# A two-layer graph network: wide product in the setup, rows broadcast by loads, the Rayleigh quotient on VectorE, one convolution moved to the drain between the layers, and a new order of the last batches

## What is computed

```python
h = relu(layernorm(x));  x = x + L0(h, adj)
h = relu(layernorm(x));  x = x + L1(h, adj)

def L0(x, adj):                      # 8 Euler steps, linear in h
    h = x @ fc_in_w.T + fc_in_b
    for _ in range(8):
        f = sigmoid(alpha) * 0.5 * (adj @ h - h) + h @ (w * clip(d, 0, 1) @ w.T) - h + x0
        h = h + f / 8
    return h

def L1(x, L, adjacency):
    lam_max = eigvalsh(L)[-1] + 1e-8
    h = relu(layernorm(((2 * L / lam_max - I) @ x) @ Wc + bc)) + x
    q, k, v = h @ Wq, h @ Wk, h @ Wv          # 4 heads of 32
    attn = softmax(where(adjacency > 0, q @ k.T / sqrt(32), -1e9))
    x2 = layernorm(h + (attn @ v) @ Wo + bo)
    return layernorm(x2 + gelu(x2 @ W1 + b1) @ W2 + b2)
```

## Time and profile before

| | us |
|---|---|
| median of 3 runs | 900.57 (898.94 to 904.41) |
| the profiled execution | 900.85 |
| its span, first to last instruction | 899.0 |
| PE busy | 850.9 (95%) |
| PEld busy | 715.9 (80%) |
| DVE busy | 649.3 (72%) |
| ACT busy | 539.1 (60%) |
| POOL busy | 327.2 (36%) |

### The profile page before, as it was taken

How to read it: one execution, slowest core, us unless ns; L and a number is a source line. 1 busy time by engine, 2 the same in 40 slices (tenths; PEclk the granted TensorE clock), 3 DMA queues, 4 the chain that set the end, 5 groups by cost and what they waited for, 6 DMA issues and landing times.

```text
span 899.0 us, 19047 instructions
## 1 busy us (share of the span) xinstructions
PE 850.9 (95%) x6765; PEld 715.9 (80%) x6765; DVE 649.3 (72%) x2110; ACT 539.1 (60%) x1234; POOL 327.2 (36%) x426
## 2 busy tenths in 40 slices
PE   6999999999999999988999999999999999989993
PEld 5779999999999888986777777777777777767873
DVE  6865555545453545635889999999999988987996
ACT  3134343434343232314888888988888888886884
POOL 3211111111111132301444455555555454424986
PEclk9799999999999999999999999999999999999997
DMA  3000000000000000230555554344455555410122
GB/s 103 0 1 25 12 12 13 12 13 13 12 12 13 12 24 1 76 66 3 139 143 142 142 141 127 105 119 123 98 140 143 141 142 137 112 37 1 48 71 71
DMA packets 46429, 61.73 MB, mean 69 GB/s; under 512 B 3568, under 2 KB 21247, under 8 KB 46335
## 3 DMA queue, kind: packets, MB, share of 16 engines
q1 hardware_dynamic: 46034, 60.38, 26.0%
q10 hardware_dynamic: 300, 0.13, 0.1%
HBM read 39.53 MB, written 20.97 MB: 67 GB/s over the span
## 4 chain that ended last, share of the span: by engine, by line
PE 29%; DVE 11%; issue 6%; ACT 4%; DMA 3%; SPq 1%; POOL 0%; DVEq 0%; ACTq 0%; POOLq 0%
PE bank L1769 7%; PE bank L1789 5%; PE bank L1831 4%; PE bank L1756 4%; DVE prob L1938 3%; PE bank L1509 3%; PE bank L1491 2%; DMA q_stack<-bounce_k 2%; ACT prob L1881 2%; PE bank L359 1%; DVE z_std L308 1%; DVE probT L1925 1%; PE bank L363 1%; DVE stats_b L285 1%; PE bank L1472 1%
## 5 line engine op out<-in xcount | busy, mean ns | idle before, releaser
L1881 ACT ACTIVATE prob<-prob,low 128x512 f32<-128x512 f32 x256 | 184.0, 719 | 31.0 <-DVE low L1938 29.0
L1938 DVE CUSTOM_DVE_ANT_0 prob<-bank,mask 128x512 f32<-128x512 f32 x256 | 171.0, 683 | 10.0 <-PE bank L1756 7.6
L1769 PE MATMUL bank<-ident,prob 128*128 128x128 f32 x1024 | 157.6, 276 | 1.0 <-ACT probT L1864 0.8
L1769 PEld LDWEIGHTS bank<-ident,prob 128*128 128x128 f32 x1024 | 120.6, 141 | 40.5 <-issue 29.2
L1756 PE MATMUL bank<-k_stack,q_stack 128*128 128x512 f32 x256 | 124.1, 486 | 9.8 <-DVE low L1938 8.0
L1864 ACT ACTIVATE probT<-bank 128x512 f32<-128x512 f32 x176 | 103.7, 589 | 21.7 <-PE bank L1769 21.5
L820 PE MATMUL bank<-B_hi,halves 128*128 128x384 f32 x384 | 107.2, 342 | 1.6 <-DVE halves L1183 1.1
L791 PE MATMUL bank<-halves,P3T_hi 128*128 128x256 f32 x512 | 95.4, 288 | 3.4 <-DVE halves L1201 2.2
L610 POOL TENSOR_SCALAR var_eps<-mv 128x4 f32<-128x4 f32 x16 | 3.6, 226 | 243.7 <-DVE mv L1127 243.7
L791 PEld LDWEIGHTS bank<-halves,P3T_hi 128*128 128x128 f32 x512 | 81.7, 194 | 5.8 <-DVE halves L1201 2.5
L820 PEld LDWEIGHTS bank<-B_hi,halves 128*128 128x128 f32 x384 | 70.7, 189 | 4.6 <-DVE halves L1183 2.0
(11 more groups left out here) (265 smaller groups left out, 1994.0 us busy)
## 6 DMA issues: line engine op xcount, KB each, us to landing
k_stack<-bounce_q SPq DMA_DIRECT2D x64, 256.0 KB, 4.6
q_stack<-bounce_k SPq DMA_DIRECT2D x64, 256.0 KB, 7.6
bounce_q<-k_parts SPq DMA_DIRECT2D x16, 512.0 KB, 2.8
bounce_k<-q_parts SPq DMA_DIRECT2D x16, 512.0 KB, 3.0
x_in<-in_x_dram SPq DMA_DIRECT2D x16, 256.0 KB, 2.8
out_dram<-probT SPq DMA_DIRECT2D x16, 256.0 KB, 2.3
y<-in_adj_dram SPq DMA_DIRECT2D x4, 256.0 KB, 3.7
W1s<-in_L_gnn_W_dram SPq DMA_DIRECT2D x1, 128.0 KB, 2.3
```

Source lines behind the costliest of these rows:

```text
L1769: last = pe.transpose(psum[2 + u % 2][:, mt * P:(mt + 1) * P], prob[u % RING][:, mt * P:(mt + 1) * P], ident[:, :])
L1881: act.activation(prob[u % RING][:, :], prob[u % RING][:, :], ACT.Exp, bias=low[:, u % TURNED:u % TURNED + 1], scale=-1.0, accum_out=row_su ...
L1938: dve.tensor_tensor_reduce(prob[u % RING][:, :], psum[u % 2][:, :], mask[:, u // HEADS, :], 1.0, 3e38, ALU.add, ALU.min, low[:, u % TURNED ...
```

## The change

Six edits, made together. (1) P2 is made product by product (all hi*hi of the four tiles, then hi*lo, then lo*hi), so that it can start before the rests of P are there; half of the rounding of P moves from ACT to DVE; S is added up later; POOL's sum `PT` is gone. (2) U starts as the columns 0, 1 and row sum, and is split; PE multiplies it as a weight of 3 columns with `PT_hi` and `PT_lo` (12 matmuls of 512 columns), which gives all three rows at once. (3) The nine vectors are loaded by DMAs that read the row for each of the 128 partitions. (4) S*v goes to VectorE: DVE writes v on four diagonals, PE with a weight of ones turns that into v on all partitions, DVE multiplies each tile of S with it and sums; all of it in pair 5. (5) The convolution of batch 2 is done in pair 8, in f32, and not in round 1; `v_product` of batch 0 goes to pair 7. (6) At the end DVE takes `z3_moments(15)` ahead of `finish(13)`, and POOL makes the last `y_be3` one batch earlier.

```diff
@@ the loads (SP)
-                        sp.dma_start(one.row_in[:, n, :], row.rearrange("(o d) -> o d", o=1)
+                        sp.dma_start(one.bc_all[:, n, :], row.rearrange("(o d) -> o d", o=1).broadcast_to([P, D])
@@ GpSimd: setup and pair
-                pool.wait_ge(PT_lo_ready, NT)
-                pool.tensor_tensor(out=PT[:, :, :], in0=PT_parts[0][:, :, :].bitcast(F32), ...
-                    if p == LAM_PAIR:
+                    x_and_bias(2 * p, 0)
+                    if p == LAM_PAIR - 1:
                         for b in range(2):
                             h_scales(pool, one, b, b)
-                    x_and_bias(2 * p, 0)
@@ TensorE: P2, the sums of rows, the spread rows
-                pe.wait_ge(Pn_lo_ready, NT)
-                pe.wait_ge(PT_lo_ready, NT)
-                for mt in range(NT):
-                    node_power(mt, PT_parts, P2_psum)
+                pe.wait_ge(Pn_hi_ready, NT // 2)
+                pe.wait_ge(P_ready, 2 * NT + NT // 2)
+                pe.wait_ge(PT_hi_ready, NT)
+                for n, (left, right) in enumerate(products(Pn_parts, PT_parts)):
+                    for mt in range(NT):
...
                 pe.wait_ge(S_ready, 2)
                 pe.wait_ge(B_step, 1)
                 pe.matmul(SQ_BANK[:, 0:1], ones[:, :], row_sum[:, :], start=True, stop=True).then_inc(setup_psum, 1)
-                pe.wait_ge(PT_sum_ready, 1)
-                pe.wait_ge(U_ready, 2)
-                for nt in range(NT):
-                    for k in range(NT):
-                        last = pe.matmul(psum[6][:, nt:nt + 1], PT[:, k, nt * P:(nt + 1) * P], U[:, k, 1:2], ...
+                pe.wait_ge(U_ready, GROUP + 2)
+                for k in range(NT):
+                    for n, (u, p) in enumerate(products(U_parts, PT_parts)):
+                        last = pe.matmul(psum[6][0:GROUP, :], u[:, k, :], p[:, k, :], ...
-                pe.wait_ge(one.rows_loaded, 16 * ROWS)
-                for c in range(3):
-                    pe.matmul(psum[4 + c][:, 0:cols], ones[0:1, :], row_flat[:, c * N:c * N + cols], ...
@@ TensorE: early
-                    if step == (0, "T1a"):
-                        pe.wait_ge(square_ready, NT * SQUARINGS)
+                    if step == (-1, "T1b"):
+                        pe.wait_ge(Sv_step, NT)
                         for nt in range(NT):
-                            for k in range(NT):
-                                last = pe.matmul(SQ_BANK[:, nt:nt + 1], S[:, k, nt * P:(nt + 1) * P], v[:, k:k + 1],
+                            last = pe.matmul(SQ_BANK[:, nt * P:(nt + 1) * P], ones[:, :],
+                                             one.convT[:, nt * P:(nt + 1) * P], start=True, stop=True)
-                    if step == (0, "Y1_0"):
-                        pe.wait_ge(Sv_step, 3)
+                    if step == (-1, "C3b"):
+                        pe.wait_ge(Sv_step, 2 * NT + 2)
-                    if step == (2, "Y1_1"):
+                    if step == (1, "Y0_1"):
                         pe.wait_ge(one.q_lo_ready, 1)
                         v_product(pe, one, SQ_BANK, 0)
+                    if step == (2, "Y1"):
+                        pe.wait_ge(one.v_copied, 1)
+                        for k in range(NT // 2):
+                            conv(pe, one, SQ_BANK, 2, 0, k)
+                    if step == (2, "Y1_1"):
+                        for k in range(NT // 2, NT):
+                            conv(pe, one, SQ_BANK, 2, 0, k)
@@ VectorE: setup
+                for t in range(NT // 2, NT):
+                    dve.tensor_copy(Pn_parts[0][:, t, :], Pn[:, t, :]).then_inc(P_ready, 1)
                 power_out(4)
-                dve.wait_ge(adjT_ready, NT)
-                dve.tensor_tensor(out=S[:, :, :], in0=A[:, :, :], in1=adjT[:, :, :], op=ALU.add)
...
-                turned_lo(0, P2T_parts, NT + 1)
+                for mt in range(NT):
+                    turned_lo(mt, P2T_parts, NT + mt + 1)
...
-                for c in range(3):
-                    dve.wait_ge(one.rows_spread, c + 1)
-                    dve.tensor_copy(one.bc_all..., psum[4 + c][:, 0:cols])
+                dve.tensor_scalar(U_rows[:, :], psum[6][0:GROUP, :], ident[0:GROUP, 0:1], None,
+                                  ALU.add).then_inc(rows_ready, 1)
@@ VectorE: early (SV_PLACES = {"T2b": (0, 1), "C0b": (2,), "C1b": (3,)})
-                    if step == (0, "T1a"):
-                        for b in range(2):
-                            y_moments(dve, one, b)
+                    if step == (-1, "y0"):
+                        y_moments(dve, one, 0)
+                    if step == (-1, "y1"):
+                        y_moments(dve, one, 1)
+                    if step == (-1, "v"):
+                        for nt in range(NT):
+                            dve.tensor_scalar(one.convT[:, nt * P:(nt + 1) * P], ident[:, :], v[:, nt:nt + 1], ...
+                    if p == LAM_PAIR - 1 and at in SV_PLACES:
+                        dve.wait_ge(lam_psum, 1)
+                        for nt in SV_PLACES[at]:
+                            dve.tensor_tensor_reduce(diagonal[...], S[:, nt, :], SQ_BANK[:, :], 1.0, 0.0, ALU.mult,
+                                                     ALU.add, Sv[:, nt:nt + 1]).then_inc(Sv_step, 1)
@@ layer 1: round 1 has no convolution and no split_h any more
-                    if within(r, 1, BATCH - 2):
+                    if within(r, 2, BATCH - 2):
                         split_h(r + 1, 1 - s)
-                        if AT_CONV <= u < AT_CONV + NT and within(r, 0, BATCH - 2):
+                        if AT_CONV <= u < AT_CONV + NT and within(r, 2, BATCH - 2):
-                            conv_out(act, one, A_BANK, r + 1)
+                            conv_out(act, one, A_BANK if r > 1 else psum[7], r + 1)
@@ the end
+        if b < BATCH - 1:
+            shifted_y(pool, b)
+        if b == BATCH - 2:
+            shifted_y(pool, b + 1)
         inverse_root(pool, b, mv3[b % 2], mv3_ready, ve3, rstd3[b % RING], pool3, z3_std_ready, b - RING + 1,
...
-                finish(dve, BATCH - 3)
                 z3_moments(dve, BATCH - 1)
-                finish(dve, BATCH - 2)
-                finish(dve, BATCH - 1)
+                for b in range(BATCH - 3, BATCH):
+                    finish(dve, b)
```

112 lines of the change are left out of this document (63 added, 49 removed).

## The result

The changed kernel takes 887.79 us (median of 4, 887.13 to 889.18), the kernel before 899.76 beside it: ratio 0.9854, 95% interval 0.9818 to 0.9889. The two profiled executions are 887.13 and 900.85, their spans 885.3 and 899.0.

What follows compares the result with a forecast made beforehand. It took PE, then DVE, then PE to bound the setup, PE layer 0's pairs, ACT round 1. Terms -3.7 + 0.9 - 6.7 + 0.9 - 1.2 - 0.8 = -10.6 from 900.85 gave 890.25, median 890.0; range 887 to 894.

Steps and rivals of the forecast that it cites:

- rival D: Whole kernel: every term comes at its good bound, -13.6 in sum, 887.0 us and somewhat below; chance 0.08.
- Setup, -3.7: Setup: first squaring 4.5 us earlier, less a third of 2.4 for a possible clock loss, so -3.7.
- bounds -2.1 and -4.9: Setup term's limits: -2.1 with the clock loss of 2.4 in full, -4.9 with none and a better chain of powers.
- Pair 5, +0.9: Pair 5 pays for the quotient's added PE and DVE work: +0.9 us, bounds 0.3 and 2.8.
- Pair 6, -6.7: Pair 6 loses S*v (3.48 us) and Y1 falls from 9.07 to 5.85: -6.7, bounds -5.5 and -6.8.
- Pair 7, +0.9: Pair 7 takes v_product, where PE has no wait to hide it: +0.9 us.
- Pair 8, 0: Pair 8: both halves of batch 2's convolution, 1.72 us each, hidden in PE's waits, with 0.4 to spare.
- Round 1, -1.2: Round 1 without batch 2's convolution: ACT goes on at 434.75, not 435.94, so -1.2, bounds -0.5 and -2.0.
- End, -0.8: End: last finish at 893.7 to 894.2, not 894.76, so -0.8 us, bounds -0.3 and -1.1.
- Loads, 0: Row loads: nine rows of 64 KB each instead of 0.5, nothing in front waits for them, cost nothing.
- B: Setup: the clock falls once or twice more, giving 891.6 or 894 us; chance 0.20.
- E: Attention rounds: round 1's change starts them in another, longer phase; slower, 911 us at 1.5 a round; chance 0.02.

Runs made afterwards that it cites:

- e2: The kernel before with only the broadcast loads of the rows in place of the spreading matmuls and their copies: 897.38 us against 901.09, ratio 0.9953.
- e3: The kernel before with only the edit of the quotient (S*v to VectorE, in pair 5): 892.68 us against 901.09, ratio 0.9901.
- e12: The changed kernel with the addition of S back in its old, early place on VectorE: 889.35 us, ratio 0.9884 to the kernel before.
- e1: The kernel before with only the edits of the setup: 896.29 us against 901.09, ratio 0.9933.
- e4: The changed kernel with v_product back in pair 8 and batch 2's convolution back in round 1: 889.56 us, ratio 0.9857 to the kernel before.
- e9: e8 with v_product back in pair 8 and batch 2's convolution back in round 1: 886.05 us, ratio 0.9844 to the kernel before.
- e10: The kernel before with only the bias product (L754) over 128 rows of weight, not 3: 902.27 us against 899.79, ratio 1.0013.
- e5: The changed kernel itself, run again in five more executions: 888.72 us against 899.62 for the kernel before, ratio 0.9865.
- e7: The changed kernel with batch 15's y_be3 behind its own roots and its moments ahead of three finishes: 887.00 us, ratio 0.9855 to the kernel before.
- e6: The changed kernel with the bias product (L754) over 128 rows of weight, 125 of them zeros, not 3: 885.82 us, ratio 0.9842 to the kernel before.
- e8: The changed kernel with the edits of both e6 and e7: 883.40 us against 899.79 for the kernel before, ratio 0.9816.
- e11: The changed kernel with three one-row spreading matmuls put back ahead of P3, their results unread: 888.83 us, ratio 0.9875 to the kernel before.

## Why the prediction was right or wrong

*The time.* 890.0 was forecast, and 887.8 came (888.4 over nine executions); the range 887 to 894 holds them. The side was right. The gain was forecast as 10.6, and it is 12.0 between the medians and 13.7 between the profiled executions. That is close to the 887.0 of rival D, but not for D's reason: round 1 and the end stayed far from its good bounds (-0.44 and -0.53, against -2.0 and -1.1), and what made up for them came mostly from a fall that no term held.

*Setup, -3.7: the failed step.* Its mechanics held almost to the row. From the products of powers to the 36 steps I had 22.4 (18.1 to 40.5), and it took 22.41 (17.70 to 40.11); to the first squaring 35.45, and it took 35.34. At the start I gave S 1.05, and P2 came 1.4 earlier (21.11 to 19.70). Of that, S is 1.16 in the row that I had read, close to my term (1.5 in the profiles of e2, e3 and e12, where PE ran at full pace by then), and the other 0.3 is PE's slow start, which happened to end earlier in the changed kernel. The step that failed is the clock's: the fall in pair 0, which costs 1.6 in the profile of the kernel before, was put at nothing, and a loss of 0.8 that did not come was put in.

First, I took a third of 2.4 as a loss, because of narrow weights and waits in the new setup. The 12 matmuls with three columns brought no fall in the eight profiles of kernels with all of the setup's edits and nothing put back (changed, e1, e4 to e9). In e12 one began under them, and as I had written of that place, the 2 us of slack took it, so the fall cost nothing. All four kernels that keep the 16 matmuls of one column (before, e2, e3, e10) have a fall that begins in the course of them or, in e10, within 1 behind them.

Second, and larger, I took the fall in P3 for the only one that concerned the setup. The kernel before has another at 66 to 70, in pair 0, behind the 3-row product of L754, and it was neither in the sum nor in the range. Whether it comes is chance as far as these runs show: the changed kernel has it in e5 and not in the first profile. Averaged over the five profiles with the new setup and the narrow bias product (e1, e4, e5, e7, changed), the transpose of batch 1 starts at 70.3; over the two with the old setup (before, e3) at 74.9. That is -4.6 for the term that I put at -3.7 and that the pair of profiles shows as -6.6.

*Setup "bounds -2.1 and -4.9".* They bound the terms that I had seen, not a fall that could vanish. To work from one profiled execution as if every other would have the same falls is the error: e1's times alone spread over 5.5.

*Pair 5, +0.9; measured +0.40*, within its bounds. L832 costs PE about what I had given it (1.05 with its drain), but the wait of 0.59 for an output of C (the prediction names rows 3 for it) is not seen in the new profile, and DVE's sums were ready when PE came to L838, so that neither of the two delays that I had added was paid.

*Pair 6, -6.7; measured -6.90*, and -6.8 in e3 alone. Y1 took 5.75 at clock 1.00. Right in size and cause: the four kernels that keep S*v with its one-column matmuls (before, e1, e2, e10) have a fall at 309 to 323 in their profiles, and none of the ten others has.

*Pair 7, +0.9; measured +0.78* (0.89 by e4 and e9; every pair is also 0.11 shorter, see below). *Pair 8, 0; measured 0.0.* I had "0.4 to spare" for the second half of the convolution, and the trace left 0.45 in both. What I had not costed is a fall that costs 1.5 and stands in four of the seven profiles without the convolution there, and in none with it. The move seems to avert it, and that would be more than its work gives and takes; shown it is not.

*Round 1, -1.2; measured -0.44.* The mechanism is right, as e6 and e8 show, where the round is 0.9 to 1.0 shorter than in e9, e3 and before; 1.2 was somewhat too much. In the changed kernel a fall at 410 to 413 stands under the products of k and q and takes 0.5 of it back; in the kernel before it stood at 418 to 421, under work with slack (28.80, against 28.81 in e3 without a fall).

*End, -0.8; measured -0.53*, and -0.3 as a mean over the five profiles with the old end and the six with the new (10.08 to 9.76). I had given 0.5 by the rule that the two engines exclude one another and 1.1 without it, and took the middle. The profile decides for the rule: beside the two `y_be3`, which take 2.94 where two alone take 2.54, DVE's two operations take 1.08 and 1.64 instead of 0.66 and 0.69; in e7 the sum beside a `y_be3` takes 1.71. This is what the Trainium skill says (SBUF — State Buffer, section Who interferes with whom): a VectorE instruction with two inputs in SBUF and a GpSimd instruction that reads SBUF contend, and the later of the two waits until the other is done. With a row that already showed it, splitting the difference was wrong.

*Loads, 0.* Nothing in the setup waited for the rows. *Rivals.* B (the clock falls once or twice more) was priced against P3 alone; what happened is its mirror, falls that went away. E (the rounds in another phase) did not come: rounds 2 on took 438.23 against 438.01.

*Open.* 0.59 between the transposes of batch 1 and of batch 11: each pair gives 0.11 to 0.12, spread over PE's stream (L820 at 0.174 a matmul instead of 0.176), in every kernel with all of the setup's edits and in none without. Where the tiles lie in SBUF has changed; nothing here tests that. And from `x1T` of round 2 to the first sum of the MLP the profiles differ by 1.6 among themselves (376.2 in e8 to 377.9 in e5) without a cause that I could name.

## What to carry to other kernels

Before a term is sized from one trace, list every stretch at the lower clock in it, whatever it was that one came to look at, and count each as a term that a change may remove, move or bring back; where the same code runs in several profiles, compare them first. A matmul of 512 columns took 0.23 here with 3 columns of weight as with 128, so narrow weights saved no time, and three of the four falls in the profile of the kernel before began under narrow ones or within 2 behind them. Padding one such weight with zero rows cost PE nothing; in four profiles the fall behind it was gone, on the changed kernel the time fell too, on the kernel before it did not. A rule that a row already supports is to be taken in full and not averaged with its opposite.

## What the hardware showed

The granted clock is not the same from execution to execution of one program: pair 0 of the changed kernel took 15.89 and 17.48 between the same two instructions, and the fall, where it came, lasted 3.4 (e5) or 6.8 (e4, whose code is the same there).

At the start PE runs at half pace with a granted clock of 1.00 in the records: four transposes of 128 columns take 1.06 up to some point and 0.60 behind it. In the changed kernel:

```profile
12.24 1.06 PE L666 MATMUL bank<-ident,y 128*128 128x128 f32 x4
13.52 0.85 PE L675 MATMUL bank<-ident,y 128*128 128x128 f32 x4
14.44 0.60 PE L675 MATMUL bank<-ident,y 128*128 128x128 f32 x4
```

That point lay between about 10 and 16 in the fourteen profiles, and the products of powers followed it: 16.2 to 16.6 where it came first (e1, e6, e8, e11), 18.2 to 18.3 where it came last (e5, e9), all with the same setup. That is up to 2 us of the spread of the times, and no edit here aims at it.
